# Cross-attention and mixture-of-experts kernel: normalised rows made on ScalarE instead of GpSimd, and the indirect scatters released by other events

## The reference, cut to what matters

```
x = x + attention(layernorm(x), ctx, ctx)      # 128 batches of 128 tokens, width 256, 16 heads of 16
x = x + ffn(layernorm(x))
layernorm(x) = (x - mean) / sqrt(var + 1e-5)   # over the 256 columns
ffn: 2 shared experts for every token; a softmax router picks 4 of 16 routed experts per token,
     gate = the 4 probabilities; each expert is 256 -> 128 -> gelu -> 256
```

## Time and profile before

| what | value |
|---|---|
| time, median of 3 runs | 3096.67 us (3094.06 to 3101.54) |
| the profiled execution, its own time | 3078.89 us |
| its span, first to last instruction | 3077.1 us |
| busy: PE / DVE / ACT / POOL | 72% / 55% / 32% / 60% |
| mean granted TensorE clock | 0.851 of full speed |
| attention phase | to about 1736 us of the span |

### The profile page before, as it was taken

How to read it: one execution, slowest core, us unless ns; L and a number is a source line. 1 busy time by engine, 2 the same in 40 slices (tenths; PEclk the granted TensorE clock), 3 DMA queues, 4 the chain that set the end, 5 groups by cost and what they waited for, 6 DMA issues and landing times.

```text
span 3077.1 us, 55896 instructions
## 1 busy us (share of the span) xinstructions
PE 2219.2 (72%) x21056; PEld 1713.7 (56%) x21056; DVE 1683.0 (55%) x4681; ACT 974.5 (32%) x1826; POOL 1843.3 (60%) x1716
## 2 busy tenths in 40 slices
PE   6888888888888888888886299999994333334331
PEld 3655556556565656655654288888894233323321
DVE  3555555554555555545554288888873544454444
ACT  2433333333333333433332155555551010101100
POOL 2355555545555555555544566666657777777776
PEclk8999988888889999999996599999997666666665
DMA  4223232222222232222222377777784555455543
GB/s 171 67 71 104 73 98 72 89 86 87 87 74 94 70 98 79 92 83 83 83 73 69 123 277 274 275 276 276 275 296 147 154 164 156 149 159 160 154 128 119
DMA packets 207370, 420.50 MB, mean 137 GB/s; under 512 B 25601, under 2 KB 124929, under 8 KB 207106
## 3 DMA queue, kind: packets, MB, share of 16 engines
q1 hardware_dynamic: 157954, 282.65, 27.5%
q0 software_dynamic: 49152, 134.28, 13.4%
HBM read 215.50 MB, written 201.33 MB: 135 GB/s over the span
## 4 chain that ended last, share of the span: by engine, by line
PE 39%; POOL 20%; DVE 17%; issue 9%; another core or an unknown queue 9%; ACT 6%; DMA 1%; POOLq 0%; DVEq 0%; SPq 0%; ACTq 0%
POOL gb L1004 19%; PE A L382 5%; PE A L355 5%; PE A L433 4%; PE A L450 4%; PE A L549 4%; PE A L533 3%; ACT pr L593 3%; PE A L472 3%; DVE mx L682 3%; PE A L437 3%; DVE xl L866 3%; PE A L516 3%; PE A L465 2%
## 5 line engine op out<-in xcount | busy, mean ns | idle before, releaser
L967 POOL DMA_INDIRECT xs<-xn,idx x512 | 502.1, 981 | 695.5 <-PE A L450 305.5
L1004 POOL DMA_INDIRECT gb<-ys,idx x512 | 587.6, 1148 | 174.3 <-issue 174.3
L516 PE MATMUL A<-ident,xr 128*128 128x128 f32 x1408 | 209.7, 298 | 472.7 <-DVE xl L866 421.4
L516 PEld LDWEIGHTS A<-ident,xr 128*128 128x128 f32 x1408 | 180.2, 154 | 512.8 <-issue 446.0
L593 ACT ACTIVATE pr<-A 128x512 f32<-128x512 f32 x512 | 264.4, 603 | 551.7 <-PE A L437 280.6
L900 DVE SCALAR_TENSOR_TENSOR ob<-gb,gw,ob 128x256 f32<-128x256 f32 x512 | 205.6, 479 | 416.3 <-DMA gb<-ys,idx 404.0
L682 DVE TENSOR_REDUCE mx<-A 128x4 f32<-128x512 f32 x512 | 316.7, 680 | 178.3 <-remote 125.8
L615 ACT ACTIVATE xh<-A 128x512 fp32r<-128x512 f32 x352 | 194.0, 599 | 365.9 <-PE A L516 198.6
L621 ACT ACTIVATE act<-A 128x512 f32<-128x512 f32 x208 | 124.2, 598 | 528.3 <-PE A L533 261.9
L989 POOL TENSOR_TENSOR hl<-act,hh 128x512 fp32r<-128x512 f32 x144 | 187.2, 1300 | 146.8 <-DVE hh L871 146.8
L549 PE MATMUL A<-wt,hh 128*128 128x256 f32 x1152 | 241.7, 293 | 0.0
(11 more groups left out here) (158 smaller groups left out, 4616.8 us busy)
## 6 DMA issues: line engine op xcount, KB each, us to landing
xr<-xs SPq DMA_DIRECT2D x144, 512.0 KB
ys<-yo SPq DMA_DIRECT2D x144, 512.0 KB, 3.9
xb<-in_x SPq DMA_DIRECT2D x32, 512.0 KB
cg<-in_ctx_t SPq DMA_DIRECT2D x32, 512.0 KB
yd<-xb SPq DMA_DIRECT2D x32, 512.0 KB, 3.1
x2d<-xn SPq DMA_DIRECT2D x32, 512.0 KB, 3.3
xr<-x2d SPq DMA_DIRECT2D x32, 512.0 KB
yr<-yd SPq DMA_DIRECT2D x32, 512.0 KB
```

The costliest lines, as they stand in the source:

```text
L516: ins = tr(banks[c][:, q * P:(q + 1) * P], xr[t % 3][:, q, c * P:(c + 1) * P], ident[:, :])
L967: q.indirect_dma_start(xs, bass.IndirectOffsetOnAxis(ap=idx[:, n, k:k + 1], axis=0), x2[g % 4][:, i, :], None).then_inc(sent[g % 4], 16)
L1004: q.indirect_dma_start(gb[p][:, i, k, :], None, ys, bass.IndirectOffsetOnAxis(ap=idx[:, n, k:k + 1], axis=0)).then_inc(got[p], 16)
```

## The change

GpSimd no longer makes xn and x2. It makes, from the mean and the reciprocal deviation, a bias (minus mean times reciprocal), with two more small instructions per normalisation. ScalarE makes the tiles with four ACTIVATE instructions each, scale and bias taken per partition: `NA1(g+2)` at i = 2 of the list, behind the copy of PV; `NA2(g-1)` at i = 0, behind the copy of OT. The waits that stood before the tiles go with them. GpSimd now waits, before it overwrites the small tiles, for ScalarE's last use of them. The four scatters of a batch in the list wait for S(n), PV(n-1), OT(n-1) and ST(n): the second and third events are one batch earlier than before, and the fourth is the transposed scores at the end of batch n-1 instead of OP(n). In the list the fourth scatter stands behind ST(n+1).

```diff
+        out += [("S", n + 1), ("SC", s), first, ("PV", n), ("SC", s + 1)]
+        if i == 2:
+            out.append(("NA1", g + 2))
+        out += [second, ("OTR", n), ("MT", n + 1), ("OT", n), ("SC", s + 2)]
+        if i == 0:
+            out.append(("NA2", g - 1))
+        out += [third, ("OP", n), ("ST", n + 1), ("SC", s + 3)]
...
+            def NA1(g):                                  # ScalarE
+                act_e.wait_ge(ln1_rs, g + 1)
+                if g > 0:
+                    wait_filled(act_e, 1, "XT", g - 1)
+                    wait_filled(act_e, 2, "XT", g - 1)
+                for i in range(GT):
+                    ac(xn[:, i, :], xb[g % 4][:, i, :], ACT.Identity, bias=nb1[:, i:i + 1], scale=rs1[:, i:i + 1])\
+                        .then_inc(xn_ready, 1)
...
             def LN1(g):                                  # GpSimd
                 pool.wait_ge(ln1_mv, g + 1)
+                wait(pool, xn_ready, GT * g)
                 q.tensor_scalar(ve1[:, :], mv1[:, :, 1], EPS, None, ALU.add).then_inc(ln1_ve, 1)
-                pool.wait_ge(ln1_ve, g + 1)
-                q.tensor_tensor(rs1[:, :], ve1[:, :], neg_half[:, :], ALU.pow).then_inc(ln1_rs, 1)
...
-                for i in range(GT):
-                    q.tensor_scalar(xn[:, i, :], xb[g % 4][:, i, :], mv1[:, i, 0:1], rs1[:, i:i + 1],
-                                    ALU.subtract, ALU.mult).then_inc(xn_ready, 1)
+                q.tensor_scalar(ng1[:, :], mv1[:, :, 0], -1.0, None, ALU.mult).then_inc(ln1_ve, 1)
+                pool.wait_ge(ln1_ve, 2 * (g + 1))
+                q.tensor_tensor(rs1[:, :], ve1[:, :], neg_half[:, :], ALU.pow).then_inc(ln1_pw, 1)
+                pool.wait_ge(ln1_pw, g + 1)
+                q.tensor_tensor(nb1[:, :], ng1[:, :], rs1[:, :], ALU.mult).then_inc(ln1_rs, 1)
...
                 if at < B:
-                    b, stage_of, m = ((3, "S", at), (5, "PV", at), (7, "OT", at), (0, "OP", at))[k]
+                    b, stage_of, m = ((3, "S", at), (5, "PV", at - 1), (7, "OT", at - 1), (7, "ST", at))[k]
```

More of the change, by code:

```diff
@@ L38, in attention_steps @@
 def attention_steps():
-    out = [("LN1", 0), ("XT", 0), ("K0", 0), ("K1", 0), ("Q0", 0), ("Q1", 0), ("VA", 0), ("VB", 0), ("VA", 1), ("VB", 1),
-           ("LN1", 1), ("XT", 1), ("S", 0), ("MT", 0), ("ST", 0)]
+    out = [("LN1", 0), ("NA1", 0), ("XT", 0), ("K0", 0), ("K1", 0), ("Q0", 0), ("Q1", 0), ("VA", 0), ("VB", 0), ("VA", 1), ("VB", 1),
+           ("LN1", 1), ("NA1", 1), ("XT", 1), ("S", 0), ("MT", 0), ("ST", 0)]
     for n in range(B):
@@ L49, in attention_steps @@
         s = TOPK * (n - 2 * GT - 1)
-        out += [("S", n + 1), ("SC", s), first, ("PV", n), ("SC", s + 1), second, ("OTR", n), ("MT", n + 1), ("OT", n),
-                ("SC", s + 2), third, ("OP", n), ("SC", s + 3), ("ST", n + 1)]
+        out += [("S", n + 1), ("SC", s), first, ("PV", n), ("SC", s + 1)]
[5 more added lines that the diff above has]
+        out += [third, ("OP", n), ("ST", n + 1), ("SC", s + 3)]
         out += after
     g = G
-    out += [("RK", g - 2), ("R2", g - 2), ("XT2", g - 1), ("RL", g - 1), ("R1", g - 1), ("RK", g - 1), ("R2", g - 1)]
+    out += [("RK", g - 2), ("R2", g - 2), ("NA2", g - 1), ("XT2", g - 1), ("RL", g - 1), ("R1", g - 1), ("RK", g - 1), ("R2", g - 1)]
     out += [("SC", k) for k in range(TOPK * (B - 2 * GT - 1), TOPK * B)]
@@ L158, in program @@
         st1, mv1, ve1, rs1 = sa("st1", [P, GT, 6]), sa("mv1", [P, GT, 2]), sa("ve1", [P, GT]), sa("rs1", [P, GT])
+        ng1, nb1, ng2, nb2 = (sa(k, [P, GT]) for k in ("ng1", "nb1", "ng2", "nb2"))
         st2, mv2, ve2, rs2 = sa("st2", [P, GT, 6]), sa("mv2", [P, GT, 2]), sa("ve2", [P, GT]), sa("rs2", [P, GT])
@@ L205, in program @@
         ln1_st, ln1_mv, ln1_ve, ln1_rs, xn_ready = sem("ln1_st"), sem("ln1_mv"), sem("ln1_ve"), sem("ln1_rs"), sem("xn_ready")
+        ln1_pw, ln2_pw = sem("ln1_pw"), sem("ln2_pw")
         m_hi, m_lo = sem("m_hi"), sem("m_lo")
@@ L607, in R1, with NA2 @@
                 ac(ex[:, :, :], ls[:, :, :], ACT.Exp).then_inc(r_exp, 1)
+            def NA1(g):
[6 more added lines that the diff above has]
+                        .then_inc(xn_ready, 1)
+            def NA2(g):
+                act_e.wait_ge(ln2_rs, g + 1)
+                wait(act_e, sent[g % 4], 16 * TOPK * GT * (g // 4))
+                wait(act_e, x2_kept[g % 4], 16 * (g // 4))
+                if g == 3:
+                    act_e.wait_ge(zeroed, 16 * NRT)
+                for i in range(GT):
+                    ac(x2[g % 4][:, i, :], xb[g % 4][:, i, :], ACT.Identity, bias=nb2[:, i:i + 1], scale=rs2[:, i:i + 1])\
+                        .then_inc(xn2_ready, 1)
             act_e.wait_ge(const_set, 1)
-            run(ATT, {"K0": K0, "K1": K1, "Q0": Q0, "Q1": Q1, "XT": XT, "XT2": XT2, "ST": ST, "PV": PV, "OT": OT, "R1": R1})
+            run(ATT, {"NA1": NA1, "NA2": NA2, "K0": K0, "K1": K1, "Q0": Q0, "Q1": Q1, "XT": XT, "XT2": XT2, "ST": ST, "PV": PV, "OT": OT, "R1": R1})
             def TR(t):
@@ L661, in LN1 @@
                 dve.wait_ge(ln1_st, g + 1)
-                wait(dve, xn_ready, GT * g)
+                wait(dve, ln1_rs, g)
                 for i in range(GT):
@@ L711, in LN2 @@
                 dve.wait_ge(y_ready, GT * (g + 1))
-                wait(dve, xn2_ready, GT * g)
+                wait(dve, ln2_rs, g)
                 for i in range(GT):
@@ L929, in LN1 @@
                 pool.wait_ge(ln1_mv, g + 1)
+                wait(pool, xn_ready, GT * g)
                 q.tensor_scalar(ve1[:, :], mv1[:, :, 1], EPS, None, ALU.add).then_inc(ln1_ve, 1)
-                pool.wait_ge(ln1_ve, g + 1)
-                q.tensor_tensor(rs1[:, :], ve1[:, :], neg_half[:, :], ALU.pow).then_inc(ln1_rs, 1)
[L933 to L936, removed]
-                for i in range(GT):
-                    q.tensor_scalar(xn[:, i, :], xb[g % 4][:, i, :], mv1[:, i, 0:1], rs1[:, i:i + 1],
-                                    ALU.subtract, ALU.mult).then_inc(xn_ready, 1)
+                q.tensor_scalar(ng1[:, :], mv1[:, :, 0], -1.0, None, ALU.mult).then_inc(ln1_ve, 1)
[3 more added lines that the diff above has]
+                q.tensor_tensor(nb1[:, :], ng1[:, :], rs1[:, :], ALU.mult).then_inc(ln1_rs, 1)
             def LN2(g):
                 pool.wait_ge(ln2_mv, g + 1)
+                wait(pool, xn2_ready, GT * g)
                 q.tensor_scalar(ve2[:, :], mv2[:, :, 1], EPS, None, ALU.add).then_inc(ln2_ve, 1)
[L944 to L953, removed]
+                q.tensor_scalar(ng2[:, :], mv2[:, :, 0], -1.0, None, ALU.mult).then_inc(ln2_ve, 1)
+                pool.wait_ge(ln2_ve, 2 * (g + 1))
+                q.tensor_tensor(rs2[:, :], ve2[:, :], neg_half[:, :], ALU.pow).then_inc(ln2_pw, 1)
+                pool.wait_ge(ln2_pw, g + 1)
+                q.tensor_tensor(nb2[:, :], ng2[:, :], rs2[:, :], ALU.mult).then_inc(ln2_rs, 1)
             def SC(s):
```

## The result

| | before | after |
|---|---|---|
| time, median of 4 | 3099.1 us (3094.1 to 3108.6) | 3139.6 us (3137.5 to 3140.7) |
| ratio, 95% interval | 1 | 1.0126 (1.010 to 1.015) |
| profiled span | 3077.1 us | 3138.9 us |
| busy PE / DVE / ACT / POOL | 72 / 55 / 32 / 60% | 72 / 53 / 35 / 50% |
| granted clock, 300 to 1400 us of the span | 0.91 | 0.87 |

The kernel became 1.3% slower where 4% faster was forecast. GpSimd did lose its tiles (60% to 50% busy), and TensorE has the same work, but its clock is lower and its list takes longer.

A forecast was written before the change was run, and what follows sets the result against it. TensorE's ordered list, lengthened by scatters holding ST, bounds the attention phase. Terms of 21.5, 47, 4, 36, 5.5 and 8.6 take 122.6 us off 3078.9; with the 17.8 us profile-to-run difference, 2974 us, range 2935 to 3095.

The forecast's parts named there:

- the first rival: Scatter trains hold PV as well, at i = 1 (54 us) and i = 0 (26 us): 3054 us; chance 0.20.
- the sign named against the forecast: PV's copy, or the exponentials after i = 0, staying 0.9 us behind the last of four scatters would show the forecast wrong.
- The holding itself: GpSimd's scatter trains hold ST to their end; freeing ST at i = 3 gains 0.74 us a group, 21.5 us.
- PV at i = 0: Part of the first rival: the train behind LN2 costs late groups some 2 us beyond the idle 1.43, 26 us.
- PV at i = 1: Part of the first rival: the train on `idx` covers PV, costing 2.7 us in 10 groups and 1.4 in 19, 54 us.
- i = 1 to i = 2: From OP of i = 1 to the exponentials after i = 2: 1.67 us gained in 28 groups, 47 us.
- End of i = 0: ST at the end of i = 0 meets only the scatter on `idx`, or none: 36 us gained over the groups.
- ScalarE's tiles: Four activations per normalisation on ScalarE, taken at 1.6 us, bounded by 2.06, fit its idle time and cost nothing.
- `gm`: VectorE's `gm`, 386 ns in the median under LN2's tiles, would fall to 195 ns: 5.5 us gained.
- Start and end: First tiles 1.3 us earlier, second group's 2.7 us, last 36 scatters 4.6 us: 8.6 us together.
- second rival: ST at the end of i = 0 caught by four scatters, 6.8 us a group: 3097 to 3171; chance 0.13, few groups 0.09.
- third rival: Scatters do not hold ST, both only lie behind OP; only 5.5 and 8.6 us remain: 3083 us; chance 0.04.

The follow-up runs named there:

- version with i = 0 alone corrected: Changed kernel with only the four scatters of batch i = 0 of each group waiting for PV of that batch: 3068.0 us, ratio 0.991.
- three and one: Changed kernel with a batch's first three scatters released by PV of their own batch, the fourth by ST of the next: 2820.6 us, ratio 0.916.
- tiles alone: Changed kernel with the old scatter events and the fourth scatter's old place, leaving only the tiles' move to ScalarE: 3014.2 us, ratio 0.963.
- only the fourth moved: Changed kernel with the first three scatters at their old events, the fourth released by ST of the next batch and placed behind it: 2869.4 us, ratio 0.931.
- the best: Changed kernel with three scatters released by PV of their own batch and one by ST of the next: 2820.6 us, ratio 0.916.

## Why the prediction was wrong

The step that failed is the one that took PV at no cost in the sum and left it to the first rival, at 0.20 and 80 us. That rival's mechanism is the answer, and the sign named against the forecast is there: PV's copy starts 0.94 us behind the last of four scatters. But its price was too low: PV costs 140 us net, at i = 0, 1 and 3. Between the gain of 122.6 us in the sum and the loss of 61.8 us lie 184 us; PV is 140 of them, and gains that stayed under their size are the other 44.

- **The holding itself** was read rightly: a stage in strips is held to the end of a chain, and OP and transposes are not. ST at the end of i = 3 went from 2.26 to 1.52 us, 21.6 us in sum where 21.5 stood. At i = 1 it was 24.4 us.
- **PV at i = 0** I had at some 2 us in late groups only, 26 us, hidden elsewhere by TensorE's idle 1.43 us. It is 4.3 us in 28 of the 30 groups (8.2 against 3.9), 121 us, of which 63 return behind PV. The chain ran from exp + 2.4 to + 7.3, which is OP + 3.9 to + 8.8 where 3.4 to 8.3 was forecast; I counted what the next stage could absorb as if only its idle time were lost. The version with i = 0 alone corrected gives 82 us for it.
- **PV at i = 1** I had at 54 us; it is 65, with 9 given back.
- **PV at i = 3** (+36 us, with 11 given back) stood nowhere. No chain meets it. The granted clock is 0.72 there, after the stall of i = 2. Exp to osb is 5.53 us, and 3.05 in the version with three and one, which has no stall at i = 2 and a single scatter at the same place.
- **i = 1 to i = 2**, 47 us and 4 for the last group: from OP of i = 1 to the exponentials after i = 2 the time fell by 24.5 us. The last two groups gave 1.7 and 2.2 of it, each of the others 0.73 and not 1.67 us. The chain of seven started 2.49 and not 2.27 us after the epsilon, and the exponential followed it after 1.67 instead of 0.89 us. The 0.89 held only for the chains of five of the kernel before, where ST's matmuls were issued in time.
- **End of i = 0**, 36 us: 24.1. ST is at half clock in 28 of 30 groups now, where it was in 18, with PV's stall before it. My argument that less stall would give a better clock was right in kind, but the stall grew.
- **ScalarE's tiles** took 2.06 us for four, the upper bound and not my 1.6, and cost nothing, as forecast: the version with tiles alone gains 3.7%.
- **`gm`**, 5.5 us: this did not come. The tiles of LN2 no longer hold it, but a scatter of the chain in front of PV does, and it ends with that scatter's record, within 5 ns in 29 groups. Its median rose from 386 to 427 ns. With tiles alone the next scatter starts just behind it, and it is 195 ns.

```profile
1161.44 0.96 POOL L986 DMA_INDIRECT xs<-xn,idx  x1 [0.30 <-issue]
...
1161.97 0.43 DVE L771 TENSOR_SCALAR gm<-rest 128x64 bf16<-128x64 f32 x1
...
L771 DVE TENSOR_SCALAR gm<-rest x32: 194/427/432, 131.8 to 1760.6; 128x64 bf16<-128x64 f32 x32
```

- **Start and end**, 8.6 us: 3.5 + 4.1 = 7.6 measured.
- The **second rival** (ST caught at the end of i = 0) did not occur: OP to exp fell there from 3.55 to 2.75 us in the mean. The slower side came through PV, which I had priced only as a smaller gain.
- The **third rival** is refuted by the run with arithmetic in the scatters' place (0.912).

The run with arithmetic agrees with the port rule weighed in the prediction (the Trainium skill, "SBUF — State Buffer", section "Who interferes with whom"): GpSimd's arithmetic does not hold TensorE. But that section names no way at all for GpSimd to hold up TensorE, and the indirect DMAs are one, at 4.3 us a PV of i = 0.

**What stays open.** Why matmuls on 32-row or 32-column strips are held, and transposes and OP on the whole array not. The trace shows both forms of it, a late result (PV of i = 0) and late issue (ST of i = 2). That both use strips is what sets them apart here, and the router's short matmuls speak against shortness as such; but no run had PV or ST without strips, so it is argued and not shown. No run had a gather in the scatters' place. Whether S is held was not measured by itself.

## What to carry to other kernels

When a background operation holds one stage up, ask which other stages have the same weakness before you move it: here the chains of four between the exponentials and PV cost 115 us net at i = 0 and 1, more than the 76 us that the move gave behind OP, while a single scatter there cost nothing. Release such operations by a fresh event, just behind the last sensitive stage; events long past let an in-order queue that was blocked discharge everything at once. And price a stall with the clock that it takes down in the batch behind it (36 us at i = 3).

## What the runs showed of the hardware

- An indirect DMA of 128 rows on GpSimd (0.96 us, 1.27 apart in a chain) holds PV and ST, which use strips of the array. In chains of four to seven their result comes 0.9 to 1.7 us after the last one's end; behind one or two it comes after 0.3 to 0.7 us (0.50 in the earlier trace rows, 0.32 in the earlier trace rows, 0.68 at PV of i = 3 with only the fourth moved). It is the same at 64 bytes a row as at 1 KB. Plain DMAs of the same size from the same queue (0.54 us each) and arithmetic (0.71 us each) do not.
- A single one costs nothing if it ends 1.2 us before PV's copy would start (952.15 against 953.35).
- It holds a VectorE instruction too: `gm` takes 427 ns beside a scatter and 195 ns without, and ends with the scatter's record.
- Four ACTIVATEs of 128x256 from SBUF with scale and bias per partition take 2.06 us.
- The granted clock between 300 and 1400 us followed the stalls: 0.87 in the kernel after, 0.91 before, 0.94 with tiles alone, 0.97 in the best.
